# A new order of the attention stage's side work, and expert chunks of 352 and 288 rows

## The chip, the cores and the metric

The kernel runs on one core of one Trainium2 chip. Its time is the device time of one execution in microseconds (us), from the first to the last instruction and what lies around them; three runs gave 522.79, 523.56 and 525.09 us, median 523.56 us. Smaller is better.

## The reference

One block of a network on 16 sequences of 128 tokens with 256 features (2048 tokens), all in float32:

1. Sliding-window cross-attention: `x = x + tanh(g_xattn) * attention(layernorm(x), ctx, ctx)`. It has 16 heads of width 16. The tokens are read as two runs of 1024 in blocks of 128; a query sees keys of its own block and the one before, in a band of 129.
2. A mixture of experts: `x = x + tanh(g_ffn) * experts(layernorm(x))`. A router of 8 experts gives each token its two most probable ones. Each expert takes at most 640 of its tokens, in order, and computes `y = (silu(x W_g) * (x W_u)) W3` with 1024 hidden units; the results go back to the tokens, weighted by the router's probability.

```
logits = clip(xn @ Wr.T); probs = softmax(logits); top_p, top_i = top_k(probs, 2)
rank   = position of the token among those of its expert;  kept = rank < 640
gu = einsum('ecd,efd->ecf', buf, W12);  h = silu(g) * u
y  = einsum('ecf,edf->ecd', h, W3)
out[token] += y_slot * weight
```

For the inputs used, the reference's router sends 225, 328, 984, 337, 706, 204, 671 and 641 rows to experts 0 to 7. Four experts (0, 1, 3, 5) have fewer than 352 rows; the other four have more than 384 and fill all 640 slots. These are called light and heavy experts below.

## The kernel before, in words

Every engine has its own program, written out by hand in the order in which it runs; semaphores join them. There is no scheduler. The order of the calls in each `body` is the order of the instructions.

**Attention** (the first 200 us). Eight bodies, n = 0 to 7, treat two sequences each. A body has eight groups, g = 0 to 7, of four heads. The line numbers are those of the kernel before.

- TensorE computes `scores` (a mask matmul, L1306, and three fp32r products, L1309, into bank `S[g % 2]`), then transposes the probabilities of two groups earlier (`prob_columns`, L1319), then weighs the values of three groups earlier (`weigh_values`, L1333). `scores` of a group waits until ScalarE has done the exponentials of two groups earlier, since the bank is shared.
- VectorE takes the negated maximum of each row (`largest`, tile `nm`, L942), makes the low half of the probabilities (`low_probs`, tile `pT`, L947), and sums and scales the heads' output (`heads_out`, L956 and L958; `heads_scale`, tile `oN`, L966).
- ScalarE computes the exponentials (`exps`, tile `p`, four per group, L633) and the high half of the probabilities (`high_probs`, tile `pT`, L640).

Between these, each group has one piece of side work that belongs to another body: the next body's normalized inputs (`xn`, `xT`), keys (`k`), queries (`q`) and values (`vf`, `V`); the output projection of the body before (`oN` transposed by `output_columns`, L1341; copied to `oT`, L626; `project_out`, L1347); and layernorm and routing of the body before that (`x2_columns`, L1273 on TensorE, L587 on ScalarE, tile `xnT`; `logits`, L1281; the small VectorE operations from `clip_logits` to `slots`, whose end is `late`, `slot`, `pslot`, `slotu`, L925 to L937). Two banks serve all of it: `Xo` (outputs, x2, logits, ranks) and `Xp` (inputs, keys, queries, values). GpSimd runs the second layernorm (tile `xr`, L455 to L462) beside it and scatters the routed rows to memory with indirect DMAs.

**Experts** (from 227 us on). Expert e is done in one or two chunks of rows, `CHUNKS = ((0, 384), (384, 256))`. `up` computes for each of eight groups f of 128 hidden units two products (gate and up) over two halves of the features, each in three fp32r passes (high*high, low*high, high*low): 12 matmuls per f, 96 per chunk, the rows being the moving operand, so that each is 384 or 256 columns wide. ScalarE takes silu (L762), VectorE the product `hF` (L1162), ScalarE the high half `hH` (L742), VectorE the low half `hL` (L1166). `down` computes 128 rows of the output: the hidden values are the stationary operand, 128 columns of them, and W3 is the moving one, 256 wide; 24 matmuls for each tile t of rows. Meanwhile the next expert's weights are split into high and low halves (L727, L1133) and its rows transposed (`rows_columns`, L1481). `weigh` (L1183) scales a tile into `ysc`, and GpSimd adds it to the output with an indirect DMA (L549).

The second chunk runs only if the expert has more rows than the first chunk holds; a bit in `flags` says so, and each engine branches on it (`pe.If` at L1558).

## Time and profile before

| | us |
|---|---|
| median of three runs | 523.56 |
| the profiled execution, its own time | 523.19 |
| its span, first to last instruction | 521.3 |
| TensorE busy (matmul) | 478.3, 92% |
| VectorE busy | 351.9, 68% |
| ScalarE busy | 295.3, 57% |
| GpSimd busy | 189.6, 36% |

The span has three parts: attention to about 205 us, the last routing and the first rows' transposes to about 227 us, and the eight experts to 510 us, with the last addition behind them. Matmuls overlap, and the row of one gives its modelled length; how fast they follow each other is read from the starts of neighbouring rows. TensorE's granted clock is in the row PEclk, in tenths of full speed.

### The profile page before, as it was taken

What the parts mean: (1) busy time and instruction counts of PE and PEld (TensorE: products, weight loads), DVE (VectorE), ACT (ScalarE), POOL (GpSimd) and SP (SyncE); (2) the same over time, 40 slices, a digit from 0 to 9 for tenths busy, and PEclk for the clock granted to TensorE, in tenths of its full rate; (3) what the DMA queues carried; (4) which work ended last, traced back from release to release, by engine and by line L of the source; (5) the groups of instructions that cost most, each with busy time, mean ns of one, the idle gap of its engine ahead of it and who ended that gap; (6) DMA issues with size and microseconds to landing.
All of it is one profiled execution on the core that took longest, in us unless ns stands there. A gap on an engine that the chain in (4) does not pass through costs nothing.

```text
span 521.3 us, 10673 instructions
## 1 busy us (share of the span) xinstructions
PE 478.3 (92%) x3566; PEld 441.9 (85%) x3588; DVE 351.9 (68%) x864; ACT 295.3 (57%) x747; POOL 189.6 (36%) x257
## 2 busy tenths in 40 slices
PE   4899999999999886399999999999999999999991
PEld 3677888887878764399899999999999999999991
DVE  5697888889797997648776764675844858534340
ACT  5877878687778771427564643565633737324140
POOL 7527546686867576500303030112022030310302
PEclk9999999999999997589999999999999999999997
DMA  5999232414233511172757460465532464200111
GB/s 163 258 221 263 61 42 63 98 47 83 60 65 82 195 51 62 52 265 82 233 175 189 139 183 10 82 220 100 211 59 29 129 190 131 31 11 11 15 16 20
DMA packets 41650, 57.34 MB, mean 110 GB/s; under 512 B 3721, under 2 KB 38576, under 8 KB 39552
## 3 DMA queue, kind: packets, MB, share of 16 engines
q1 hardware_dynamic: 35008, 48.49, 31.9%
q0 software_dynamic: 6144, 8.07, 9.2%
q8 instruction: 28, 0.46, 0.4%
q10 hardware_dynamic: 448, 0.14, 0.2%
q14 instruction: 22, 0.18, 0.1%
HBM read 36.24 MB, written 16.72 MB: 102 GB/s over the span
## 4 chain that ended last, share of the span: by engine, by line
PE 56%; DVE 2%; issue 1%; DMA 0%; POOL 0%; another core or an unknown queue 0%; ACT 0%; DVEq 0%; POOLq 0%
PE bank L1487 18%; PE bank L1489 17%; PE bank L1488 17%; PE bank L1481 2%; PE bank L1415 1%; DMA expert_rows<-xr,slotu 0%; PE bank L1281 0%; POOL out_tokens L549 0%; PE bank L1273 0%; DVE xr L843 0%; DVE ysc L1183 0%; DVE xr L841 0%; DVE topi L884 0%; PE bank L1466 0%
## 5 line engine op out<-in xcount | busy, mean ns | idle before, releaser
L549 POOL DMA_INDIRECT out_tokens<-ysc,rows x32 | 49.8, 1558 | 243.9 <-DVE ysc L1183 237.3
L1487 PE MATMUL bank<-bXh,wh 128*128 128x384 f32 (+1 forms) x384 | 121.9, 318 | 1.5 <-issue 1.2
L1489 PE MATMUL bank<-bXh,wl 128*128 128x384 f32 (+1 forms) x384 | 121.8, 317 | 0.0
L1488 PE MATMUL bank<-bXl,wh 128*128 128x384 f32 (+1 forms) x384 | 121.8, 317 | 0.0
L762 ACT ACTIVATE sil<-bank 128x384 f32<-128x384 f32 (+1 forms) x96 | 43.8, 456 | 126.6 <-PE bank L1489 126.5
L1162 DVE TENSOR_TENSOR hF<-sil,bank 128x384 f32<-128x384 f32 (+1 forms) x96 | 49.0, 510 | 76.2 <-ACT sil L762 74.0
L633 ACT ACTIVATE p<-bank,nm 128x128 f32<-128x128 f32 x256 | 73.7, 384 | 25.1 <-DVE nm L942 25.0
L1487 PE MATMUL bank<-wh,hH 128*128 128x256 f32 x256 | 73.8, 288 | 0.3 <-DVE ysc L1183 0.3
L1488 PEld LDWEIGHTS bank<-bXl,wh 128*128 128x128 f32 x384 | 72.7, 189 | 1.3 <-issue 1.3
L1487 PEld LDWEIGHTS bank<-bXh,wh 128*128 128x128 f32 x384 | 72.7, 189 | 0.5 <-issue 0.5
L1489 PEld LDWEIGHTS bank<-bXh,wl 128*128 128x128 f32 x384 | 72.6, 189 | 0.0
L1489 PE MATMUL bank<-wh,hL 128*128 128x256 f32 x256 | 72.4, 283 | 0.0
L1488 PE MATMUL bank<-wl,hH 128*128 128x256 f32 x256 | 72.4, 283 | 0.0
L1309 PE MATMUL bank<-kM,q 128*128 128x512 f32 x192 | 67.0, 457 | 0.0
L1133 DVE TENSOR_TENSOR wl<-stage,wh 128x512 fp32r<-128x512 f32 x96 | 63.1, 685 | 3.1 <-ACT wh L727 1.6
L727 ACT ACTIVATE wh<-stage 128x512 fp32r<-128x512 f32 x96 | 56.6, 622 | 1.4 <-DMA stage<-in_w3T 1.4
L1487 PEld LDWEIGHTS bank<-wh,hH 128*128 128x128 f32 x256 | 49.0, 191 | 1.3 <-DVE ysc L1183 0.7
L942 DVE TENSOR_REDUCE nm<-bank 128x4 f32<-128x512 f32 x64 | 43.5, 680 | 8.6 <-PE bank L1309 8.5
L1166 DVE TENSOR_TENSOR hL<-hF,hH 128x384 fp32r<-128x384 f32 (+1 forms) x96 | 48.7, 507 | 0.7
L1488 PEld LDWEIGHTS bank<-wl,hH 128*128 128x128 f32 x256 | 49.1, 192 | 0.0
L1489 PEld LDWEIGHTS bank<-wh,hL 128*128 128x128 f32 x256 | 49.0, 192 | 0.0
L742 ACT ACTIVATE hH<-hF 128x384 fp32r<-128x384 f32 (+1 forms) x96 | 46.3, 482 | 0.9 <-DVE hF L1162 0.9
(144 smaller groups left out, 815.9 us busy)
## 6 DMA issues: line engine op xcount, KB each, us to landing
stage<-in_w12T SPq DMA_DIRECT2D x16, 1024.0 KB
stage<-in_w3T SPq DMA_DIRECT2D x8, 1024.0 KB
expert_rows<-padrow SPq DMA_DIRECT2D x8, 662.5 KB, 8.9
rows<-expert_rows SPq DMA_DIRECT2D x7, 662.5 KB, 4.2
kM<-k SPq DMA_DIRECT2D x62, 64.0 KB, 2.4
cT<-in_ctxT SPq DMA_DIRECT2D x8, 256.0 KB, 3.3
out_tokens<-x_all SPq DMA_DIRECT2D x8, 256.0 KB
x_all<-in_x SPq DMA_DIRECT2D x2, 640.0 KB, 5.6
```

The source lines that it names most:

```text
L549: pool.indirect_dma_start(out=out, out_offset=bass.IndirectOffsetOnAxis(rows[par][:, c, D + E:ROW].bitcast(U32), 0), in_=ysc[par][:, c, :] ...
L633: ins = act.activation(p32[g % 2][:, h, :], S[g % 2][:, h * T:(h + 1) * T], ACT.Exp, bias=nm[g % 2][:, h:h + 1])
L727: act.activation(Wh[par][:, k, q * QW:(q + 1) * QW], stage[s][:, q * QW:(q + 1) * QW], ACT.Copy)\
L742: act.activation(hH[c][:, f, :], hF[j % 2][:, 0:w], ACT.Copy).then_inc(act_hh, 1)
L762: act.activation(sil[j % 2][:, 0:w], Gb[j % 2][:, 0:w], ACT.Silu).then_inc(act_sil, 1)
L1133: dve.tensor_tensor(Wl[par][:, k, cols], stage[s][:, cols], Wh[par][:, k, cols].bitcast(F32), ALU.subtract)\
L1162: dve.tensor_tensor(hF[j % 2][:, 0:w], sil[j % 2][:, 0:w], Ub[j % 2][:, 0:w], ALU.mult).then_inc(dve_h, 1)
L1166: dve.tensor_tensor(hL[c][:, f - 1, :], hF[jj % 2][:, 0:w], hH[c][:, f - 1, :].bitcast(F32), ALU.subtract)\
L1309: ins = nc.tensor.matmul(S[g % 2][:, :], q2[par][:, sq, hq // 2, b * T:(b + 1) * T], kM[par][:, sk, GH * hq:GH * hq + GH, b * T:(b + 1) * ...
L1487: nc.tensor.matmul(out_ap, ah, bh, start=start, stop=False)
L1488: nc.tensor.matmul(out_ap, ah, bl, start=False, stop=False)
L1489: return nc.tensor.matmul(out_ap, al, bh, start=False, stop=stop)
```

## The change

Two independent edits.

**Order in the attention bodies.** On TensorE, `output_columns` of the body before moves from the end of group 0 to behind the scores of group 1, and `project_out` behind `weigh_values` of group 1. On VectorE, `low_probs` comes ahead of `heads_out`, and in group 0 ahead of `largest`; `keys_low` comes ahead of `largest` of group 3; the small router operations are spread anew, with `gate_columns` behind `slots`. On ScalarE, the keys move from group 3 (ahead of its exponentials) to group 2 (behind them), `x2_columns` behind these, `values1` from group 7 to the next body's group 0, and `values2` to group 1. The tile `slot` now lies in bank `Xo` in place of SBUF, so TensorE's next use of that bank waits for one operation more (`pslot`).

**Chunks.** `CHUNKS` becomes 352 and 288 rows; transposes and splits of the rows keep 384 and 256 (`TILED`). `hH` and `hL` become one tensor each. The third tile of rows straddles the chunks: a light expert computes its first 96 rows, with 96 stationary columns, and a heavy one computes all 128 after its second `up`. TensorE's branch now asks for fewer rows first.

```diff
-CHUNKS = ((0, 384), (384, 256))
+CHUNKS = ((0, 352), (352, 288))
+TILED = ((0, 384), (384, 256))
+SPLIT = 2
+REST = CHUNKS[0][1] - SPLIT * P
 # GpSimd, after the scatters
+            pool.memset(ysc[0][REST:P, SPLIT, :], 0.0).then_inc(spare_ok, 1)
+            pool.memset(ysc[1][REST:P, SPLIT, :], 0.0).then_inc(spare_ok, 1)
 # ScalarE, body
-                    if g == 7 and nxt:
-                        values(n + 1, Xp)
-                        values1(n + 1, 1 - par)
                     if (cur and g >= 2) or (prev1 and g < 2):
                         high_probs(G - 2, g % 2, not prev1 and g < 4)
                     if g == 0 and prev1:
+                        values1(n, par)
                         output_columns(SB * (n - 1), Xo)
-                    elif g == 2 and prev2:
-                        x2_columns(n - 2, Xo)
-                    elif g == 3 and nxt:
-                        keys(n + 1, Xp)
+                    elif g == 7 and nxt:
+                        values(n + 1, Xp)
                     if cur:
                         exps(G, g, not prev1 and g < 2)
...
+                    elif g == 2 and nxt:
+                        keys(n + 1, Xp)
+                    if g == 2 and prev2:
+                        x2_columns(n - 2, Xo)
 # VectorE, slots
-                dve.scalar_tensor_tensor(slot[:, a:b, :], late[:, a:b, :], LATE, rk, ALU.mult, ALU.add).then_inc(dve_rk, 1)
+                slot = bank[:, 2 * SB * E:2 * SB * E + (b - a) * E].rearrange("p (j e) -> p j e", e=E)
+                dve.scalar_tensor_tensor(slot, late[:, a:b, :], LATE, rk, ALU.mult, ALU.add).then_inc(dve_rk, 1)
 # TensorE, body
+                    if g == 1 and prev1:
+                        if prev3:
+                            pe.wait_ge(dve_rk, R_SLOT * (n - 3) + 3)
...
+                        output_columns(SB * (n - 1), Xo)
                     if (cur and g >= 2) or (prev1 and g < 2):
                         prob_columns(G - 2, g % 2, not prev1 and g < 4)
 # TensorE, expert
-                output_bank(e, 2, first)
-                down(e, par, 0, 2, range(FT))
-                with pe.If(more_rows(flags, e)):
+                with pe.If(fewer_rows(flags, e)):
+                    output_bank(e, SPLIT, first)
+                    down(e, par, 0, SPLIT, range(FT), REST)
+                with pe.Else():
                     up(i, par, 1, first)
-                    for t in range(CT0, CT):
+                    for t in range(SPLIT, CT):
                         output_bank(e, t, first)
                         down(e, par, 1, t, range(FT))
```

Three places show the moved instructions. The first is TensorE from group 0 to group 2 of an even body; `kM,q_0` are scores, `ident,p` the transposed probabilities, `ident,oN` the `output_columns`, `wo,oT` the projection. Before:

```order
L1309 MATMUL bank<-kM,q_0 128x512 x3
L1319 MATMUL bank<-ident,p_0 128x128 x4
L1234 MATMUL bank<-ident,xn 128x128 x4
L1333 MATMUL bank<-V_1,pT 128x50 x8
L1341 MATMUL bank<-ident,oN 128x128 x2
L1306 MATMUL bank<-causal,identb 128x512
L1309 MATMUL bank<-kM,q_0 128x512 x3
L1319 MATMUL bank<-ident,p_1 128x128 x4
L1347 MATMUL bank<-wo,oT 128x256 x2
L1333 MATMUL bank<-V_1,pT 128x50 x8
```

The same stretch of TensorE in the changed kernel, to the projection:

```order
L1327 MATMUL bank<-kM,q_0 128x512 x3
L1337 MATMUL bank<-ident,p_0 128x128 x4
L1252 MATMUL bank<-ident,xn 128x128 x4
L1351 MATMUL bank<-V_1,pT 128x50 x8
L1324 MATMUL bank<-causal,identb 128x512
L1327 MATMUL bank<-kM,q_0 128x512 x3
L1359 MATMUL bank<-ident,oN 128x128 x2
L1337 MATMUL bank<-ident,p_1 128x128 x4
L1351 MATMUL bank<-V_1,pT 128x50 x8
L1365 MATMUL bank<-wo,oT 128x256 x2
```

The transposes of `oN` now stand behind the next scores, and the projection behind the weighing.

The second place is VectorE from `largest` of group 7 to that of the next body's group 0 (`nm` is `largest`, `pT` is `low_probs`, `osum` to `oN` the heads, `late` to `slotu` the slots). Before:

```order
L942 TENSOR_REDUCE nm<-bank 128x4
L956 TENSOR_REDUCE osum<-bank 128x128
L958 RECIPROCAL bank<-bank 128x8
L966 TENSOR_TENSOR oN<-osum,bank 128x128
L947 SCALAR_TENSOR_TENSOR pT<-bank,pT 128x512
L925 TENSOR_TENSOR late<-bank,limit 128x16
L929 SCALAR_TENSOR_TENSOR slot<-late,bank 128x16
L931 TENSOR_TENSOR pslot<-pick,slot 128x32
L937 TENSOR_REDUCE slotu<-pslot 128x4
L942 TENSOR_REDUCE nm<-bank 128x4
```

And VectorE in the changed kernel, from the same `largest` on:

```order
L959 TENSOR_REDUCE nm<-bank 128x4
L964 SCALAR_TENSOR_TENSOR pT<-bank,pT 128x512
L973 TENSOR_REDUCE osum<-bank 128x128
L975 RECIPROCAL bank<-bank 128x8
L983 TENSOR_TENSOR oN<-osum,bank 128x128
L941 TENSOR_TENSOR late<-bank,limit 128x16
L946 SCALAR_TENSOR_TENSOR bank<-late,bank 128x16
L948 TENSOR_TENSOR pslot<-pick,bank 128x32
L954 TENSOR_REDUCE slotu<-pslot 128x4
L918 SCALAR_TENSOR_TENSOR xr<-lex,tg,lrc 128x2x8
L964 SCALAR_TENSOR_TENSOR pT<-bank,pT 128x512
L959 TENSOR_REDUCE nm<-bank 128x4 x2
```

`low_probs` moved ahead of the heads, `gate_columns` (`xr<-lex`) came in, and one more `low_probs` stands ahead of the next `largest`.

The third place is ScalarE in groups 2 and 3 (`pT` is `high_probs`, `p` the exponentials). Before:

```order
L640 ACTIVATE pT<-bank 128x512
L587 ACTIVATE xnT<-bank 128x512
L633 ACTIVATE p_0<-bank,nm 128x128 x4
L640 ACTIVATE pT<-bank 128x512
L606 ACTIVATE k<-bank,bqkv 128x256 x2
L633 ACTIVATE p_1<-bank,nm 128x128 x4
```

And in the changed kernel:

```order
L654 ACTIVATE pT<-bank 128x512
L647 ACTIVATE p_0<-bank,nm 128x128 x4
L620 ACTIVATE k<-bank,bqkv 128x256 x2
L601 ACTIVATE xnT<-bank 128x512
L654 ACTIVATE pT<-bank 128x512
L647 ACTIVATE p_1<-bank,nm 128x128 x4
```

The keys come one group earlier, and `xnT`, which the logits of group 3 read, now stands behind the exponentials and the keys.

## Rows read from the trace of the kernel before

**Rows 1.** The page: busy share of TensorE, and its granted clock in 40 slices.
```profile
PE 478.3 (92%) x3566; PEld 441.9 (85%) x3588; DVE 351.9 (68%) x864; ACT 295.3 (57%) x747; POOL 189.6 (36%) x257
PEclk9999999999999997589999999999999999999997
```
**Rows 2.** The page: the chain that ended last, by line.
```profile
PE bank L1487 18%; PE bank L1489 17%; PE bank L1488 17%; PE bank L1481 2%; PE bank L1415 1%; DMA expert_rows<-xr,slotu 0%; PE bank L1281 0%; POOL out_tokens L549 0%; PE bank L1273 0%; DVE xr L843 0%; DVE ysc L1183 0%; DVE xr L841 0%; DVE topi L884 0%; PE bank L1466 0%
```
**Rows 3.** Windows: length; busy us of PE, PEld, DVE, ACT, POOL; clock, DMA share, GB/s.
```profile
30.00:197.00 167.00, 159.10 (x1321) 132.76 (x1338) 142.36 (x396) 127.57 (x375) 108.01 (x144) 1.00 0.40 99
...
282.35:326.17 43.82, 43.82 (x325) 43.64 (x324) 25.57 (x53) 20.53 (x48) 8.61 (x6) 1.00 0.42 107
326.17:352.69 26.52, 26.52 (x181) 26.36 (x180) 18.46 (x35) 14.90 (x32) 3.73 (x4) 1.00 0.52 156
```
**Rows 4.** Groups by line and form, TensorE, 227 to 511 us.
```profile
L1487 PE MATMUL bank<-bXh,wh 128*128 128x384 f32 x256 | 85.7, 335 | 1.5 <-issue 1.2 <-DVE bXl L1140 0.3
...
L1487 PE MATMUL bank<-bXh,wh 128*128 128x256 f32 x128 | 36.2, 283 | 0.0
```
**Rows 5.** Timeline, TensorE, 384 columns; eleven rows of the same kind left out.
```profile
259.06 0.33 PE L1487 MATMUL bank<-bXh,wh 128*128 128x384 f32 x1
...
261.14 0.33 PE L1487 MATMUL bank<-bXh,wh 128*128 128x384 f32 x1
```
**Rows 6.** Timeline, TensorE, 256 columns (`down`); eleven rows left out.
```profile
307.09 0.28 PE L1487 MATMUL bank<-wh,hH 128*128 128x256 f32 x1
...
308.53 0.28 PE L1487 MATMUL bank<-wh,hH 128*128 128x256 f32 x1
```
**Rows 7.** Groups by line and form: VectorE's work in an expert.
```profile
L1133 DVE TENSOR_TENSOR wl<-stage,wh 128x512 fp32r<-128x512 f32 x96 | 63.1, 685 | 3.1 <-ACT wh L727 1.6 <-POOL lnv L539 1.4
...
L1162 DVE TENSOR_TENSOR hF<-sil,bank 128x384 f32<-128x384 f32 x64 | 35.5, 554 | 50.4 <-ACT sil L762 48.3 <-issue 2.1
L1166 DVE TENSOR_TENSOR hL<-hF,hH 128x384 fp32r<-128x384 f32 x64 | 35.3, 552 | 0.1
```
**Rows 8.** Groups by line and form: weight loads, fp32r (`down`) and fp16.
```profile
L1487 PEld LDWEIGHTS bank<-wh,hH 128*128 128x128 f32 x256 | 49.0, 191 | 1.3 <-DVE ysc L1183 0.7
...
L1333 PEld LDWEIGHTS bank<-V,pT 128*128 128x128 f16 x512 | 21.2, 97 | 11.5 <-DVE pT L947 6.0 <-issue 1.9
```
**Rows 9.** Timeline, TensorE: behind the first expert's branch.
```profile
257.50 0.33 PE L1487 MATMUL bank<-bXh,wh 128*128 128x384 f32 x1 [1.17 <-issue]
```
**Rows 10.** Waits, 30 to 197 us: us in total, times, longest.
```profile
PE bank L1333 <- DVE pT L947: 3.6, 7, 0.9
DVE k L979 <- ACT k L606: 6.6, 6, 1.1
ACT p L633 <- DVE nm L942: 24.1, 21, 2.0
```
**Rows 11.** Timeline where body 3 passes to 4, four engines.
```profile
106.29 0.38 PE L1333 MATMUL bank<-V,pT 128*128 128x50 bf16 x8 [0.54 <-DVE pT L947]
...
106.51 0.73 POOL L460 TENSOR_TENSOR xr<-xr,gab 128x256 f32<-128x256 f32 x1
106.55 0.73 DVE L931 TENSOR_TENSOR pslot<-pick,slot 128x32 f32<-128x32 f32 x1
...
107.42 0.68 DVE L942 TENSOR_REDUCE nm<-bank 128x4 f32<-128x512 f32 x1
...
108.14 1.15 ACT L633 ACTIVATE p<-bank,nm 128x128 f32<-128x128 f32 x4 [0.70 <-DVE nm L942]
...
109.38 1.04 PE L1309 MATMUL bank<-kM,q 128*128 128x512 f32 x3
```
**Rows 12.** Timeline, ScalarE, groups 2 and 3 of that body.
```profile
113.06 0.60 ACT L587 ACTIVATE xnT<-bank 128x512 f32<-128x512 f32 x1 [0.74 <-issue]
...
115.10 0.83 ACT L606 ACTIVATE k<-bank,bqkv 128x256 fp32r<-128x256 f32 x2
```
**Rows 13.** Waits of the whole span: TensorE's queries for VectorE's keys.
```profile
PE bank L1243 <- DVE k L979: 1.7, 2, 0.9
```

More of the change, by code:

```diff
@@ L131, in gated_block @@
         late = sb(pa, "late", [P, SB, E], F32)
-        slot = sb(pa, "slot", [P, SB, E], F32)
         pslot = sb(pa, "pslot", [P, K, SB, E], F32)
@@ L327, in _ @@
                 sp.wait_ge(scattered[s], 16 * K * SEQS // 2)
-            for (o, w), done in zip(CHUNKS, (ld_rows[0], ld_rows_rest)):
+            for (o, w), done in zip(TILED, (ld_rows[0], ld_rows_rest)):
                 if o > 0:
@@ L539, in _ @@
             pool.memset(lnv[:, :], 1.0).then_inc(pool_sent, 1)
+            for done in scattered:
+                pool.wait_ge(done, 16 * K * SEQS // 2)
+            pool.wait_ge(pool_sent, 1)
+            pool.memset(ysc[0][REST:P, SPLIT, :], 0.0).then_inc(spare_ok, 1)
+            pool.wait_ge(spare_ok, 1)
+            pool.memset(ysc[1][REST:P, SPLIT, :], 0.0).then_inc(spare_ok, 1)
+            pool.wait_ge(spare_ok, 2)
             pool.wait_ge(st_x2, 16 * NSB)
@@ L667, in body @@
                         queries(n + 1, 1 - par, Xp)
+                    if g == 4 and prev2:
+                        exps_of_logits(n - 2)
             def zero_low_keys(quarter):
@@ L1023, in body @@
                         stats1(*XCUT[g // 2:g // 2 + 2])
+                    if (cur and g >= 2) or (prev1 and g == 1):
+                        low_probs(G - 2, g % 2)
+                    if g == 4 and prev2:
+                        shift_logits(routed)
+                    elif g == 5 and prev2:
+                        sum_exps(routed)
+                    elif g == 6 and prev2:
+                        pick_experts(routed)
+                        guard_sum(routed)
+                        members(routed)
+                        invert_sum(routed)
                     if g in (1, 3) and prev1:
@@ L1031, in body @@
                         heads_scale(HPS * n + k, k, SB * n - 1 if prev1 else None)
-                    if (cur and g >= 2) or (prev1 and g < 2):
-                        low_probs(G - 2, g % 2)
-                    if g == 6 and prev2:
-                        members(routed)
-                        gate_columns(routed, par)
                     if g in (2, 6) and prev1:
@@ L1040, in body @@
                         slots(routed, par, Xo)
+                        gate_columns(routed, par)
             def zero_keys(par, part, half):
@@ L1176, in steps, with weigh @@
                         low(i + par, 1 - par, f)
-            def weigh(e, par, t, first):
+            def weigh(e, par, t, first, n=P):
                 if t == 0 and not (isinstance(e, int) and e < 2):
                     dve.wait_ge(expert_added, e - 1)
+                if t == SPLIT and isinstance(e, int) and e < 2:
+                    dve.wait_ge(spare_ok, e + 1)
                 dve.wait_ge(pe_out, CT * e + t + 1)
-                dve.tensor_scalar(ysc[par][:, t, :], Yb[(par + t) % 2][:, 0:D], rows[par][:, t, bass.ds(D + e, 1)], None, ALU.mult)\
+                dve.tensor_scalar(ysc[par][0:n, t, :], Yb[(par + t) % 2][0:n, 0:D], rows[par][0:n, t, bass.ds(D + e, 1)], None, ALU.mult)\
                    .then_inc(dve_ysc, 1)
@@ L1368, in body @@
                             values(n + 1, 1 - par, Xp)
-                    if g == 1 and prev1:
-                        project_out(SB * (n - 1), Xo)
-                    elif g == 2 and prev2:
+                    if g == 2 and prev2:
                         pe.wait_ge(dve_x2, SB * (n - 1) + 1)
@@ L1521, in up, with down @@
                     ins.then_inc(pe_gu, 1)
-            def down(e, par, c, t, parts):
-                o = t * P - CHUNKS[c][0]
+            def down(e, par, c, t, parts, n=P):
+                o = t * P
                 for f in parts:
-                    if t in (0, CT0):
+                    if t == c * SPLIT:
                         pe.wait_ge(dve_hl, 16 * e + FT * c + f + 1)
-                    ins = three(Yb[(par + t) % 2][:, 0:D],
-                                ((hH[c][:, f, o:o + P], hL[c][:, f, o:o + P]),
+                    ins = three(Yb[(par + t) % 2][0:n, 0:D],
+                                ((hH[:, f, o:o + n], hL[:, f, o:o + n]),
                                  (Wh[par][:, DC, f * D:(f + 1) * D], Wl[par][:, DC, f * D:(f + 1) * D])), f == 0, f == FT - 1)
@@ L1555, in expert @@
                     rows_columns(e + 1, 1 - par, i + 1 + par, 3)
-                output_bank(e, 2, first)
-                down(e, par, 0, 2, range(FT))
-                with pe.If(more_rows(flags, e)):
+                with pe.If(fewer_rows(flags, e)):
+                    output_bank(e, SPLIT, first)
+                    down(e, par, 0, SPLIT, range(FT), REST)
+                with pe.Else():
                     up(i, par, 1, first)
-                    for t in range(CT0, CT):
+                    for t in range(SPLIT, CT):
                         output_bank(e, t, first)
```

77 lines of the change are left out of this document (35 added, 42 removed).

## The prediction, made before the changed kernel ran

> **What bounds the kernel now.** I read the page first: TensorE is busy 92% of the span, at full clock but for two slices near the middle [rows 1], and the chain that ended last is TensorE's expert matmuls (L1487 to L1489) for over half of the span [rows 2]. Then the windows, since a mean hides stages. In a heavy expert TensorE is busy 43.82 of 43.82 us, in a light one 26.52 of 26.52, with VectorE and ScalarE far below, 18.46 and 14.90 us [rows 3]. So every nanosecond between two expert matmuls counts in full. In attention TensorE is busy 159.1 of 167 us, and VectorE 142.4 [rows 3]: these two are close, and what one waits for the other changes with the order. The waits name the joints: TensorE for `low_probs`, VectorE for ScalarE's keys, ScalarE's exponentials for the maxima [rows 10].
>
> **The chunks.** The row of a matmul (335 or 283 ns, [rows 4]) is longer than its pace; the pace is in the starts. Twelve matmuls of 384 columns take 261.14 - 259.06 = 2.08 us, 173.3 ns each [rows 5]; twelve of 256 take 308.53 - 307.09 = 1.44 us, 120 ns each [rows 6]. That is 0.4167 ns a column and a constant of 13.3 ns. Neither 352 nor 288 occurs; both lie between, so I take the line: 160 ns for 352, 133.3 ns for 288. The bounds are the neighbours: 352 can cost no more than 173.3 ns (the edit then gains nothing), and if 120 ns were a floor under a steeper line, it could be up to 7 ns less than the line says.
> - Light expert, four of them: 96 matmuls of `up` at 160 in place of 173.3 ns, 1.28 us less each, together 5.12 us.
> - Heavy expert, four: the first `up` is 96 x 13.3 = 1.28 us shorter, the second 1.28 us longer. Nothing.
> - `down`: 24 matmuls per tile before and after, with W3's 256 columns moving. For a light expert's third tile only the stationary side shrinks to 96 columns. I take the same 120 ns.
> - Does another engine stop TensorE from going faster? Per step of f it now needs 12 x 160 = 1.92 us; VectorE has hF, hL and one piece of the next weights, 554 + 552 + 685 = 1.79 us even at 384 columns [rows 7]. It fits, by 0.13 us, and more at 352.
> - The heavy third tile moves behind the second `up`. Its hidden values are ready, GpSimd's additions of 1.5 us keep pace with tiles of 24 x 120 = 2.88 us, and the tail behind the last tile is the same. Nothing. GpSimd's two clears lie in its idle time ahead of its first addition.
> - The branch: TensorE now decides ahead of the third tile. A heavy expert jumps over 24 matmuls and has only four row transposes queued to cover that (some 0.4 us). In before, a light expert jumps, under the cover of 2.9 us of queued matmuls; the first time there was nevertheless a gap of 1.17 us [rows 9], the other three had none. The bounds are 0 and 4 x (1.17 - 0.4) = 3.1 us, and below nothing about 0.5 us (the short wait for `ysc` ahead of that tile goes for heavy experts). I take 0, since a window with a jump is as full as one without [rows 3].
>
> The 96 columns are the place for a rule. A load of 128 fp32r columns shows 191 ns, one of fp16 97 ns [rows 8]: fp32r is loaded at the slow rate already. The Trainium skill, "TensorE: Matmul & The Clock Gate", on weight-path perf modes, says that the fast weight load is on when there are exactly 128 weights and the type is not FP32; by it, 96 columns would lose a fast load that 128 had. If fp32r had it, the sum would be about 2.6 us worse; by the row there is nothing to lose.
>
> **The order in attention.** Six bodies (2 to 7) have all the side work. I followed body 4 with the durations of its rows; zero is the start of its first scores, 103.8.
>
> Before, TensorE stalls 0.7 us at group 0 for `low_probs` of group 7 (0.54 visible, [rows 11]), since this stands behind the heads; 0.1 us at the scores of group 2, which follow the exponentials (108.14 + 1.15 to 109.38, [rows 11]); and 0.23, 0.15 and 0.1 us between the starts of neighbouring matmuls around the queries of group 4 and the projection of group 5. About 1.4 us a body.
>
> What goes: `low_probs` of group 7 comes about 1 us earlier, so the 0.7 us go; the keys on ScalarE end about 1 us earlier than 115.10 + 0.83 [rows 12], so VectorE's wait for them (6.6 us in six, [rows 10]) shrinks and the 0.5 us go. `pslot` took 0.73 us and ended at 107.28, just when GpSimd's L460 (106.51 + 0.73) did [rows 11]: two engines in one another's way. With `slot` in PSUM I take 0.2 us, like its neighbours.
>
> What comes: `low_probs` of group 0 (0.6 us) now stands ahead of the maxima on which ScalarE's exponentials wait. VectorE has no idle time here, so with the 0.5 us of `pslot` saved the maxima start at 3.4 to 4.1 us, against 107.42 - 103.8 = 3.6 [rows 11]. The exponentials end at 5.1 to 5.8; TensorE, no longer held at group 0, comes to the scores of group 2 at 4.6: a stall of 0.5 to 1.2 us where 0.1 was. Behind it ScalarE does `xT`, then the high half; VectorE waits for that, and the heads (1 us), formerly done in this pause, come behind it, so the maxima of group 2 end at 8.8 to 9.4. Then exponentials (1.05), keys (0.7) and only then `xnT` (0.5): it ends at 11.1 to 11.8, where the logits of group 3 would start at 10.3 to 10.9. A new stall of 0.9 us; before, `xnT` was done first, at 113.06 [rows 12], and there was none.
>
> Sum per body: 1.4 us of old stalls against 1.4 to 2.3 of new ones, 0 to +0.8; I take +0.25, times six, +1.5 us. Bodies 0 and 1 have no logits in the way and gain from the earlier keys: TensorE's queries stall 0.8 to 0.9 us in each [rows 13], most of which goes, -1.5 us. Attention together: 0, with bounds of -5 (old stalls go, the new ones stay hidden) and +5.
>
> `gate_columns` decides part of the spread. It reads two SBUF tiles, as `pslot` did, and now runs right behind `slotu`, beside GpSimd's L460 and L462; if blocked like `pslot`, it takes 0.5 us of the gain back. The Trainium skill, "SBUF — State Buffer", on the port pair that VectorE and GpSimd share, has it as an exclusive lock held for a whole instruction, taken by a VectorE operation with two SBUF inputs against a GpSimd one that reads SBUF. The rows of `pslot` agree. By this rule the upper ends above hold, +0.8 rather than 0.
>
> **Sum.** Against the profiled execution's own 523.19 us: -5.12 for the chunks, 0 for attention, 0 for the branch, 518.1. It ran 0.4 us under the median of the runs; from that median the same sum gives 518.4. I say 518.5.
>
> **Rivals.** 0.5% is 2.6 us, about what a measurement of this kernel can tell from no change: faster is below 520.9, slower above 526.2.
> - A, the forecast: chunks give 5.1 us, attention stays within 2 us. 516.5 to 520.5. Chance 0.48.
> - B, attention takes back 3 to 6 us: the logits' new wait and the later maxima show in full. For it: VectorE without idle time around the body's end, and `xnT` last in its row. Against: TensorE's old stalls do go. 521.5 to 524.5, say 522.6. Chance 0.20.
> - C, attention gains too: of 1.4 us of stalls per body 0.8 go, six times, 4.8 us. For it: VectorE's waits for keys were 1.1 us each. 513.5. Chance 0.15.
> - D, the narrow third tile or the heavy experts' jump costs 2.5 to 3 us: 521. For it the gap of 1.17 us; against it the full windows. Chance 0.11.
> - E, slower than before. Place: the scores of group 2. Mechanism: `gate_columns` is blocked, `low_probs` and maxima slip with it, TensorE waits at the weighing of group 1 (0.6), at the scores (0.6 more) and at the logits (1.0): some 2.7 us of stalls against 1.4. Six bodies, +8.1, less 5.1: 526.5. It turns slower when a body loses over 1.3 us. For it: [rows 11]; against: every term must be at its upper end. Chance 0.06.
>
> From these: faster 0.69 (A, C and half of D), same 0.25, slower 0.06. The range reaches from C's better half to B's middle, 514.0 to 522.8; A's own is 516.5 to 520.5.
>
> **What the new profile should show.** Starts of `up` matmuls 160 ns apart in first chunks and 133 in second ones; a light expert 25.2 us, a heavy one still 43.8, with no gap in front of its second `up`; `down` of the light third tile at 120 ns; `pslot` near 0.2 us; TensorE's wait for `low_probs` at group 0 gone, and waits for the exponentials at group 2 and for `xnT` at the logits in its place; bodies 23.2 to 24 us apart. I am wrong if light experts are not 1.3 us shorter, or if bodies change by more than 0.8 us.

## The result, and the profile after

The changed kernel took 528.91 us (median of six runs, 527.22 to 529.81) against 524.03 for the kernel before on the same chip: ratio 1.0091, 95% interval 1.0071 to 1.0112. It is slower; 518.5 was predicted, and the range ended at 522.8. The profiled execution took 528.68 us, with a span of 527.0 (before: 521.3).

The page of the changed kernel, busy shares and granted clock, then the chain by engine:

```profile
PE 476.7 (90%) x3588; PEld 440.1 (84%) x3588; DVE 347.2 (66%) x864; ACT 294.8 (56%) x747; POOL 190.0 (36%) x259
PEclk9999999999999997589799999998999999999997
...
PE 52%; issue 2%; DVE 2%; DMA 1%; POOL 1%; ACT 1%; another core or an unknown queue 0%; DVEq 0%; POOLq 0%
```

TensorE's share fell from 92% to 90% [rows 1], and the clock's digits have two new dips, a 7 and an 8, in the middle of the experts.

**What came as forecast.** Windows of the changed kernel, as in [rows 3]: attention, a heavy expert, a light one (expert 5).

```profile
30.00:197.00 167.00, 156.30 (x1311) 129.06 (x1309) 135.12 (x386) 126.27 (x369) 105.98 (x141) 1.00 0.40 99
286.40:330.22 43.82, 43.82 (x325) 43.75 (x323) 25.84 (x53) 20.50 (x48) 8.70 (x6) 1.00 0.43 107
404.07:429.21 25.14, 25.14 (x181) 24.99 (x179) 18.20 (x35) 14.44 (x32) 3.62 (x4) 1.00 0.54 163
```

The heavy expert is what it was, 43.82 us, and this light one 25.14 in place of 26.52. But attention is less full: 156.3 us of TensorE in 167, from 159.1. Groups by form, where [rows 4] had 384 and 256 columns:

```profile
L1505 PE MATMUL bank<-bXh,wh 128*128 128x352 f32 x256 | 84.9, 332 | 6.6 <-issue 6.3 <-DVE bXl L1156 0.3
...
L1505 PE MATMUL bank<-bXh,wh 128*128 128x288 f32 x128 | 38.0, 297 | 0.0
...
L1507 PE MATMUL bank<-wh,hL 128*96 128x256 f32 x32 | 8.9, 278 | 0.0
```

**What was not forecast** is in the first of these rows: 6.3 us of idle time with no releaser ("issue"). The timeline of TensorE shows where, behind expert 0's third tile:

```profile
254.94 0.28 PE L1506 MATMUL bank<-wl,hH 128*96 128x256 f32 x1
255.06 0.27 PE L1507 MATMUL bank<-wh,hL 128*96 128x256 f32 x1
258.50 0.63 PE L1505 MATMUL bank<-bXh,wh 128*128 128x352 f32 x1 [3.17 <-issue]
258.93 0.50 PE L1506 MATMUL bank<-bXl,wh 128*128 128x352 f32 x1
259.22 0.50 PE L1507 MATMUL bank<-bXh,wl 128*128 128x352 f32 x1
```

The same place behind expert 3:

```profile
355.32 0.27 PE L1507 MATMUL bank<-wh,hL 128*96 128x256 f32 x1
358.73 0.42 PE L1505 MATMUL bank<-bXh,wh 128*128 128x352 f32 x1 [3.13 <-issue]
```

From start to start these are 3.44 and 3.41 us, where 0.12 is normal. The matmuls behind the first gap then follow 0.29 us apart (258.93 to 259.22), not 0.16: the window behind it shows TensorE at half of its clock, 1.2 of 2.4 GHz (0.50), and the next one the way back. Behind the second gap the clock fell only 1.3 us later, so its window has a mean of 0.71.

```profile
258.50:262.00 3.50, 3.50 (x12) 3.50 (x13) 0.00 (x0) 0.00 (x0) 1.54 (x1) 0.50 0.96 274
262.00:266.00 4.00, 4.00 (x20) 4.00 (x19) 1.37 (x3) 1.65 (x4) 0.00 (x0) 0.69 0.30 69
...
358.70:362.00 3.30, 3.27 (x15) 3.28 (x16) 0.00 (x0) 0.38 (x2) 0.00 (x0) 0.71 0.36 42
```

What TensorE's sequencer did at the time stands in its branch records. They are not counted as busy, so no timeline has them; a query by source line gives their durations (ns, min/median/max). Of the changed kernel, the jumps over the long side of experts 0, 1, 3 and 5:

```profile
L1574 PEldq COMPARE_BRANCH  x1: 5226/5226/5226, 253.1 to 253.1; - x1
L1574 PEldq COMPARE_BRANCH  x1: 299/299/299, 284.3 to 284.3; - x1
L1574 PEldq COMPARE_BRANCH  x1: 4602/4602/4602, 353.4 to 353.4; - x1
L1574 PEldq COMPARE_BRANCH  x1: 174/174/174, 427.1 to 427.1; - x1
```

And all eight branches of the kernel before, with the first matmul behind the jump at 252.6:

```profile
L1558 PEldq COMPARE_BRANCH  x8: 68/148/373, 252.6 to 490.7; - x8
```
```profile
254.60 0.34 PE L1487 MATMUL bank<-bXh,wh 128*128 128x384 f32 x1
```

Two jumps take about 5 us in place of 0.3. The sequencer is some 2 us ahead of the matmuls, in the kernel before (252.6 to 254.60) as in the changed one (253.1 to 255.06): so much of a jump is covered, and the rest is the gap.

**The sum of the profiled executions**, in us. Experts: the four light ones -1.4 each, -5.5 (26.52 to 25.14; 5.1 of it are the columns), the wait for `ysc` in the last expert -0.6, the two gaps 3.3 + 3.3, the slow matmuls behind them 2.9 + 1.6 (expert 1's `up` takes 18.25, from 258.50 to 276.75, in place of 15.4, expert 4's 17.0), the old gap [rows 9] -1.4; +3.6 together. From the first expert matmul to the last it is +3.5. Attention and routing: the first expert matmul is at 229.3 in place of 227.2, +2.1. Together that is the 5.7 us of the span, to 0.1.

In attention the stalls are those that the prediction named. Waits from 30 to 197 us, as in [rows 10], then TensorE and `pslot` where body 3 passes to 4, as in [rows 11]:

```profile
PE bank L1324 <- ACT p L647: 2.1, 6, 0.4
PE bank L1299 <- ACT xnT L601: 3.9, 5, 0.8
...
PE bank L1351 <- DVE pT L964: 1.4, 3, 0.9
DVE k L996 <- ACT k L620: 4.1, 6, 0.7
```
```profile
107.08 0.19 DVE L948 TENSOR_TENSOR pslot<-pick,bank 128x32 f32<-128x32 f32 x1
...
107.41 0.23 DVE L918 SCALAR_TENSOR_TENSOR xr<-lex,tg,lrc 128x16 f32<-128x16 f32 x1
...
110.06 0.39 PE L1324 MATMUL bank<-causal,identb 128*128 128x512 bf16 x1 [0.37 <-ACT p L647]
...
116.10 0.61 PE L1299 MATMUL bank<-wr,xnT 128*128 128x8 f32 x4 [0.78 <-ACT xnT L601]
```

From start to start, 0.66 us at the scores of group 2 and 0.95 at the logits in each full body; the 0.7 us for `low_probs` are gone. A body takes 23.5 to 23.6 us where it took 23.15. The first logits already come 1.3 us later than before, at 69.04 for 67.75.

### The profile page after: what moved, and what is told of

Same layout as the page of the kernel before. It is cut to its first block, busy times and chain, and to the rows that moved or that the text cites. A ratio compares the mean times of both kernels' runs of the same rounds, so it can differ in the third digit from the quotient of the medians.

```text
span 527.0 us, 10704 instructions
## 1 busy us (share of the span) xinstructions
PE 476.7 (90%) x3588; PEld 440.1 (84%) x3588; DVE 347.2 (66%) x864; ACT 294.8 (56%) x747; POOL 190.0 (36%) x259
## 4 chain that ended last, share of the span: by engine, by line
PE 52%; issue 2%; DVE 2%; DMA 1%; POOL 1%; ACT 1%; another core or an unknown queue 0%; DVEq 0%; POOLq 0%
PE bank L1505 17%; PE bank L1506 17%; PE bank L1507 17%; PE bank L1499 1%; DMA stage<-in_w3T 1%; PE bank L1433 1%; POOL expert_rows L482 1%; ACT wh L743 0%; DVE wl L1149 0%; DMA expert_rows<-xr,slotu 0%; POOL out_tokens L563 0%; DVE osum L973 0%; DVE x_all L991 0%; DVE st L844 0%
## 5 line engine op out<-in xcount | busy, mean ns | idle before, releaser
L1505 PE MATMUL bank<-bXh,wh 128*128 128x352 f32 (+1 forms) x384 | 122.9, 320 | 6.6 <-issue 6.3
L1506 PE MATMUL bank<-bXl,wh 128*128 128x352 f32 (+1 forms) x384 | 122.3, 318 | 0.0
L1507 PE MATMUL bank<-bXh,wl 128*128 128x352 f32 (+1 forms) x384 | 122.2, 318 | 0.0
L1178 DVE TENSOR_TENSOR hF<-sil,bank 128x352 f32<-128x352 f32 (+1 forms) x96 | 47.9, 499 | 79.7 <-ACT sil L778 75.7
L1505 PE MATMUL bank<-wh,hH 128*128 128x256 f32 (+1 forms) x256 | 73.1, 286 | 0.0
L1506 PE MATMUL bank<-wl,hH 128*128 128x256 f32 (+1 forms) x256 | 72.3, 282 | 0.0
L1507 PE MATMUL bank<-wh,hL 128*128 128x256 f32 (+1 forms) x256 | 72.2, 282 | 0.0
L1505 PEld LDWEIGHTS bank<-wh,hH 128*128 128x128 f32 (+1 forms) x256 | 48.0, 188 | 0.5 <-DVE ysc L1201 0.2
L1182 DVE TENSOR_TENSOR hL<-hF,hH 128x352 fp32r<-128x352 f32 (+1 forms) x96 | 47.7, 497 | 0.7
L1506 PEld LDWEIGHTS bank<-wl,hH 128*128 128x128 f32 (+1 forms) x256 | 48.1, 188 | 0.0
```

The source lines that it names most:

```text
L1178: dve.tensor_tensor(hF[j % 2][:, 0:w], sil[j % 2][:, 0:w], Ub[j % 2][:, 0:w], ALU.mult).then_inc(dve_h, 1)
L1182: dve.tensor_tensor(hL[:, f - 1, o:o + w], hF[jj % 2][:, 0:w], hH[:, f - 1, o:o + w].bitcast(F32), ALU.subtract)\
L1505: nc.tensor.matmul(out_ap, ah, bh, start=start, stop=False)
L1506: nc.tensor.matmul(out_ap, ah, bl, start=False, stop=False)
L1507: return nc.tensor.matmul(out_ap, al, bh, start=False, stop=stop)
```

## The experiments

Each ratio is to the kernel before on the same chip, with its 95% interval.

### The two edits apart

**order_only** has the attention's hunks of the diff and none of the chunks'.

> The kernel before with the new attention order alone (with slot in PSUM), chunks and branches as before. Theory A (the order costs about 2 us, the rest of the loss is in the experts): bodies 23.5 us apart instead of 23.2, TensorE stalls 0.6 us ahead of the scores of group 2 and 0.9 us ahead of the logits, experts unchanged at 282.7 us; time 2 us above before, 525.5 to 526.5. Rival B (the order is the whole loss, since it also shifts the experts): 529.

527.77 us, ratio 1.0066 (1.0047 to 1.0086): above theory A's range and below B's 529. Its jumps are before's, its stalls those of the changed kernel (0.66 and 0.95 us a body), and its experts take 282.8 us, as before's do, so B's reason is excluded.

**chunks_only** has the chunks and the branch.

> The kernel before with the chunks of 352 and 288 and the new branches alone, attention order as before. Theory A (TensorE's jump over the long side behind a light expert's third tile finds its target not yet fetched): gaps of 3.3 us behind the third tile of experts 0 and 3, and 1.7 to 2.5 us in the up of the experts after them, as in the changed kernel; 3 to 4 us above before, 527. Rival B (the gaps come from the new attention order): no gaps, 5 us below before, 518.8.

525.04 us, ratio 1.0022 (0.9995 to 1.0050). The gaps are there, 4.08 and 3.27 us, behind jumps of 5.86 and 4.57 us. 1.0066 x 1.0022 = 1.0088: the two edits add up to the change's 1.0091, within their intervals. So the order costs some 3.5 us, and the chunks, which save 5.1 us of matmuls, give it all back at the branch; alone, they are not shown to be slower than before.

### The attention's new stalls

**xnt_first** is order_only with `x2_columns` again ahead of the exponentials of group 2:

```diff
+                    elif g == 2 and prev2:
+                        x2_columns(n - 2, Xo)
...
-                    if g == 2 and prev2:
-                        x2_columns(n - 2, Xo)
```

> The new attention order alone (order_only, 527.8), with ScalarE's copy to xnT put back ahead of the exponentials of group 2; the keys stay behind them. Theory A (xnT last in its row makes the logits wait): the 0.94 us ahead of the logits in six bodies goes; up to 5.6 us less, 522 to 524. Rival B (VectorE's and ScalarE's total work sets the pace of a body, the wait only moves): bodies still 23.5 us apart, 527.8.

**max_first** is order_only with `low_probs` of group 0 again behind `largest`:

```diff
-                    if g == 0 and prev1:
-                        low_probs(G - 2, g % 2)
                     if cur:
                         largest(G, g)
+                    if g == 0 and prev1:
+                        low_probs(G - 2, g % 2)
```

> The new attention order alone (order_only, 527.8), with low_probs of group 0 put back behind the maxima. Theory A (the maxima of group 0 are late, TensorE waits 0.6 us for the exponentials ahead of the scores of group 2): that wait shrinks by 0.5 us, the wait at the logits by as much or not at all; 2 to 5 us less, 523 to 526. Rival B (TensorE then waits for low_probs at the weighing of group 1 instead): 527 to 528.

They took 523.54 us (1.0002, 0.9987 to 1.0017) and 523.17 us (1.0003, 0.9989 to 1.0016). Each takes away one stall (the logits'; most of the scores') and is back at before's time.

**best_order** makes both edits.

> Only the attention part of the change, with two steps put back: on ScalarE the half of the layernorm's transposes (xnT) again ahead of the exponentials of group 2, and on VectorE low_probs of group 0 again behind the largest. Each of the two alone brought the kernel back to the time before (523.5 and 523.2, from 527.8). Theory: the two waits (0.95 us at the logits, 0.66 us at the scores of group 2) are separate, each was worth some 4 us, but the wait that each removal leaves (scores of group 2; weighing of group 1, 0.71 us) is the time that the other would give. With both out a body loses the old wait for low_probs only in part: 22.8 to 23.1 us a body, 521 to 522.5 us. Rival: VectorE itself sets the body by then, so both together give no more than one alone: 523 to 523.6.

523.34 us, 1.0008 (0.9992 to 1.0024): the rival. Both new stalls are gone, and the old one for `low_probs` is back, one group later. TensorE's timeline of best_order, at the weighing of group 1:

```profile
108.24 0.36 PE L1334 MATMUL bank<-V,pT 128*128 128x50 bf16 x8 [0.68 <-DVE pT L949]
```

A body takes 23.15 us, as in before, and its stalls sum to about 1.4 us in both. In the orders tried here, what VectorE and ScalarE do between two exponentials comes late somewhere, and the order chooses where; that no other order does better is not shown.

**slot_sbuf** is order_only with `slot` in SBUF again, and the new place of `gate_columns` kept:

```diff
-                slot = bank[:, 2 * SB * E:2 * SB * E + (b - a) * E].rearrange("p (j e) -> p j e", e=E)
+                slot = slot_s[:, a:b, :]
```

> The new attention order alone (order_only, 527.8), with slot back in SBUF. Theory A (two SBUF inputs make pslot wait for GpSimd's running operation): pslot 0.4 to 0.7 us again where it meets one, 0.2 where it does not, and the maxima of group 0 later by that; 0 to 3 us more, 528 to 531. Rival B (pslot's length came from its place in the order): 0.2 us, 527.8.

529.87 us, 1.0132 (1.0104 to 1.0161): 2.1 us above order_only by the medians, 3.5 by the ratios. The timeline of VectorE and GpSimd in slot_sbuf:

```profile
107.63 0.74 POOL L460 TENSOR_TENSOR xr<-xr,gab 128x256 f32<-128x256 f32 x1
...
107.95 0.46 DVE L934 TENSOR_TENSOR pslot<-pick,slot_s 128x32 f32<-128x32 f32 x1
...
108.45 0.73 POOL L462 TENSOR_TENSOR xr<-xr,beb 128x256 f32<-128x256 f32 x1
...
108.55 0.66 DVE L904 SCALAR_TENSOR_TENSOR xr<-lex,tg,lrc 128x16 f32<-128x16 f32 x1
```

`pslot` ends with GpSimd's L460 (108.41 and 108.37), and `gate_columns`, which starts 0.1 us behind L462, ends with it (109.21 and 109.18). In the changed kernel `gate_columns` starts at 107.41, ahead of the second of the two GpSimd operations (107.56), and takes 0.23 us; `pslot`, with one input in PSUM, takes 0.19 us (107.08) in the middle of the first one (106.75 to 107.48). The Trainium skill ("SBUF — State Buffer", the two sides of SBUF) has this as an exclusive lock, and the rows agree: 0.3 us for `pslot` and 0.4 for `gate_columns`, by the phase of two engines. A body takes 24.2 us in place of 23.5. Of the parts of the order that were tried alone, `slot` in PSUM is the one that pays.

### The gap: its length or its place?

**long_first** turns the branch of the changed kernel round:

```diff
-                with pe.If(fewer_rows(flags, e)):
-                    output_bank(e, SPLIT, first)
-                    down(e, par, 0, SPLIT, range(FT), REST)
-                with pe.Else():
+                with pe.If(more_rows(flags, e)):
                     up(i, par, 1, first)
...
+                with pe.Else():
+                    output_bank(e, SPLIT, first)
+                    down(e, par, 0, SPLIT, range(FT), REST)
```

A light expert now jumps over the long side ahead of its third tile, with only four transposes queued.

> The changed kernel with the long side of TensorE's branch first: a light expert jumps over it at once to its third tile, with only four transposes queued. Theory A (place of the jump's target): the jump now starts some 50 instructions earlier in the piece, so for expert 0 the target is already there: gap under 0.5 us instead of 3.4; 521 to 526. Rival B (the short side first was the better choice, since the jump is covered by 2.9 us of queued matmuls): gaps of 4 us or more at all light experts, above 530.

532.0 us, 1.0176 (1.0146 to 1.0207). The time fell on B's side, and A's gap under 0.5 us did not come; but the gaps, 4.90 and 5.78 us, are at experts 0 and 3 alone, not at all light ones. Expert 0's is the one that tells:

```profile
L1574 PEldq COMPARE_BRANCH  x1: 374/374/374, 251.5 to 251.5; - x1
```
```profile
252.95 0.28 PE L1507 MATMUL bank<-wh,hL 128*96 128x256 f32 x1
257.85 0.37 PE L1505 MATMUL bank<-wh,hH 128*96 128x256 f32 x1 [4.63 <-issue]
```

The same long jump takes 0.37 us, nine matmuls run behind its target, and then TensorE stands for 4.9 us in the middle of a tile where nothing is waited for. So it is not the jump's length alone. (Expert 3's gap stands at its jump, a record of 6.03 us.)

**split_branch** is chunks_only with `up` in an `If` of its own, so that no jump is longer than before's:

```diff
+                with pe.If(more_rows(flags, e)):
+                    up(i, par, 1, first)
                 with pe.If(fewer_rows(flags, e)):
...
                 with pe.Else():
-                    up(i, par, 1, first)
                     for t in range(SPLIT, CT):
```

> The new chunks alone (chunks_only, 525.0), with TensorE's branch in two: the second up in one If, then short or long down in another. A light expert jumps over 192 instructions, does its third tile, and jumps over 144, never over 336 at once. Theory A (a jump beyond the 16 KB pieces present waits for two fetches one after the other): no gap over 1.5 us, the time falls by 4 to 7 us, 518.5 to 521. Rival B (every light jump in the first pass costs a fetch, however far): the two gaps stay at 3 us or more, or four appear, 524 to 530.

524.79 us, 1.0023 (1.0001 to 1.0044): nothing gained, and theory A fell. Gaps of 2.67 us at experts 0 and 3, behind records of 4.45 and 3.96 us of jumps over only 148 and 158 instructions.

The two gaps are alike, and the clock behind them is not. Windows behind the first and the second:

```profile
255.40:259.20 3.80, 3.80 (x24) 3.80 (x25) 1.03 (x3) 0.98 (x2) 1.54 (x1) 1.00 0.91 268
352.20:356.00 3.80, 3.80 (x17) 3.80 (x18) 0.31 (x1) 0.97 (x2) 0.64 (x1) 0.68 0.43 55
```

So a gap of this length can cost the clock or not. That goes with the spread of one kernel's executions: of split_branch's ten, four took 522.0 to 522.8 us at a mean granted clock of 0.967 to 0.970, and six 524.6 to 526.2 at 0.960 to 0.964.

**after_pad64** is the changed kernel with code moved and nothing else: 64 matmuls of 8 columns where TensorE waits for the scatters, 128 instructions with their weight loads.

```diff
+            for _ in range(64):
+                nc.tensor.matmul(O[0][:, 0:E], onesb[:, :], member[:, 0, :], start=True, stop=True)
             for s in range(2):
                 pe.wait_ge(scattered[s], 16 * K * SEQS // 2)
```

> The changed kernel with 64 more matmuls of 8 columns (results unused) ahead of TensorE's wait for the scatters, where it sat idle for 4.3 us. Every later TensorE instruction lies 128 instructions further on in its program; the experts' instructions are the same. Theory A (where the jumps lie relative to the 16 KB pieces in which instructions are fetched decides): the gap of 3.4 us behind expert 0 goes or others appear; the jump of expert 0 takes 0.1 to 0.4 us in place of 5.2. Time between 519 and 527, and the pattern of gaps changes. Rival B (a jump behind the short side is slow for itself, or the 96 columns are): the same gaps of 3.4 us behind experts 0 and 3, 529.

527.07 us, 1.0050 (1.0021 to 1.0079), at the upper end of A's range. Expert 0's jump is fast, expert 1's now slow, and expert 3's as slow as it was (4.57 us). The window behind its gap of 3.36 us is at full clock:

```profile
L1576 PEldq COMPARE_BRANCH  x1: 346/346/346, 254.0 to 254.0; - x1
L1576 PEldq COMPARE_BRANCH  x1: 4451/4451/4451, 279.8 to 279.8; - x1
```
```profile
358.58:362.40 3.82, 3.82 (x24) 3.82 (x25) 0.85 (x2) 0.98 (x2) 0.00 (x0) 1.00 0.33 39
```

### The theory, and its two tests

The DMA part of the page has the fetching of instructions as a queue of its own, of the changed kernel:

```profile
q8 instruction: 29, 0.48, 0.4%
```

29 packets of 16,384 bytes each, so 256 instructions of 64 bytes; one comes each time TensorE enters a new piece of 256, 2 to 4 us after, so it holds the piece behind that. The places are counted in TensorE's compiled program, from its start. By these places the stall of long_first lies exactly between the weight load at place 255 of piece 15 and its matmul at place 0 of piece 16; and so does before's old gap [rows 9]. That gives the theory: the piece being run and the next one are there, and the one behind is asked for only when the next is entered; it can be run some 4.5 to 6 us later. A jump waits if it ends two pieces on, or in the next one when its own was entered less than that ago; and so does straight code that reaches a boundary too soon behind a jump. Places are counted piece.place:

| kernel, expert | jump from | into | its record, us | gap, us |
|---|---|---|---|---|
| before, 0 | 14.199 | 15.235 | 0.37 | 1.51 at 16.0 |
| changed, 0 | 14.201 | 16.30 | 5.23 | 3.44 |
| changed, 1 | 17.137 | 18.222 | 0.30 | none |
| changed, 3 | 23.53, entered 1.4 us earlier | 24.150 | 4.60 | 3.41 |
| after_pad64, 0 | 15.73 | 16.158 | 0.35 | none |
| after_pad64, 1 | 18.9, just entered | 19.94 | 4.45 | 2.87 |
| after_pad64, 3 | 23.181 | 25.22 | 4.57 | 3.36 |

The Trainium skill, "Runtime: NRT & Kernel Launch", on instruction fetch mechanics, states the blocks of 256 instructions, and that a taken branch out of a window of two forces a fetch before anything continues. The rows agree for jumps forward. The jump at the end of the loop, six pieces back, is one that the window of two does not hold, and it took 0.23 us (358.1). The page gives two sizes for TensorE's store, 2048 instructions and two blocks; the loop over experts 2 to 5 (1464 instructions) fetched 7 pieces to the end of its first pass and none in its second (no row of that queue from 363 to 437 us), which only the larger allows. Expert 5's jump, of 0.17 us, lies in that second pass.

**chunks_placed** is chunks_only with 96 such matmuls at the scatters, and 70 in expert 2's short side, which never runs with these inputs:

```diff
+                    for _ in range(spare):
+                        nc.tensor.matmul(Yb[par][:, 0:E], onesb[:, :], member[:, 0, :], start=True, stop=True)
                     down(e, par, 0, SPLIT, range(FT), REST)
...
-                expert(i, 0, False, False)
+                expert(i, 0, False, False, spare=70)
```

> The chunks and the branch of the change alone, and TensorE's code shifted: 96 tiny matmuls (8 columns) where TensorE waits for the scatters anyway, and 70 more in expert 2's short side, which never runs. Counting TensorE's program in pieces of 256 instructions, the light experts' jumps over the long side then go from place 137 of piece 15 into piece 16 (expert 0), from 73 of 18 into 19 (expert 1), and from 129 of 24 into 25 (expert 3); in the change alone they go from piece 14 into 16, 17 into 18, and from place 53 of 23, entered 1.3 us earlier, into 24. Theory of the pieces (only the next one is there, and it needs 5 to 6 us from when the one ahead of it is entered): the gaps of 4.1 and 3.3 us and the slow matmuls behind them (1.6 and 1.7 us) go, at most 1 us stays behind expert 0's jump. 516 to 518.5 us, from 525.0. Rival, the length of the jump or its being taken right behind another branch makes the gap, wherever it lies: 524 to 526.

516.31 us, ratio 0.9867 (0.9840 to 0.9893). The three jumps, and the windows behind the first and the third, at full clock:

```profile
L1575 PEldq COMPARE_BRANCH  x1: 346/346/346, 250.6 to 250.6; - x1
L1575 PEldq COMPARE_BRANCH  x1: 290/290/290, 276.1 to 276.1; - x1
L1575 PEldq COMPARE_BRANCH  x1: 281/281/281, 345.2 to 345.2; - x1
```
```profile
255.75:262.00 6.25, 6.25 (x39) 6.25 (x40) 4.56 (x10) 3.75 (x10) 2.04 (x1) 1.00 0.69 199
347.27:355.00 7.73, 7.73 (x50) 7.73 (x49) 4.44 (x9) 3.72 (x8) 2.88 (x2) 1.00 0.57 63
```

One gap is left, 0.51 us, behind the 17th matmul of expert 1's `up`, at the first places of piece 17. Code that does no work is worth 8.7 us here (525.04 to 516.31), 8.1 by the ratios. The added matmuls did nothing else that the trace shows: the first expert matmul comes at 226.75 us, in chunks_only at 226.69.

**best_placed** has the attention of best_order besides, as the whole change put right.

> The whole change with the two steps of the attention put back (best_order) and the code shifted as in chunks_placed. If both parts add up as they did in the change: best_order's time, less 5.1 us for the columns, 0.5 us for the wait for ysc and 1.4 us for the old gap behind expert 0's jump, plus 1 us for the added matmuls: 515 to 517 us. Rival, the jumps stay as slow as in the change: 523.

515.96 us, 0.9858 (0.9830 to 0.9885): the fastest, though not measurably faster than chunks_placed.

**before_pad26** tries the theory on the kernel before: the loop of after_pad64 with `range(26)`, nothing else.

> The kernel before, with nothing but 26 tiny matmuls (52 instructions) more where TensorE waits for the scatters. By the count its jumps behind expert 0 and expert 3 then end two pieces further (from place 251 of piece 14 into 16, from 208 of 22 to the first places of 24), where they ended one piece further before. Theory of the pieces: each jump's record goes from 0.35 to some 5 us, of which 2.9 us lie under queued matmuls; a gap of 2.2 us at each, and slow matmuls for 1.5 to 2 us behind it, against one gap of 1.5 us before: 528 to 531 us. Rival, only the change's longer jump or its second branch is slow: 523.5 to 524.5.

525.83 us, 1.0037 (1.0022 to 1.0051). Slower, but by less than half of what was expected, because only the first of two jumps went as the count said. The two records, then the gap behind the first and the window behind it:

```profile
L1560 PEldq COMPARE_BRANCH  x1: 5101/5101/5101, 253.7 to 253.7; - x1
L1560 PEldq COMPARE_BRANCH  x1: 340/340/340, 355.5 to 355.5; - x1
```
```profile
255.61 0.28 PE L1489 MATMUL bank<-wh,hL 128*128 128x256 f32 x1
258.97 0.41 PE L1487 MATMUL bank<-bXh,wh 128*128 128x384 f32 x1 [3.08 <-DVE wl L1133]
...
258.97:262.00 3.03, 3.03 (x13) 3.03 (x14) 0.00 (x0) 0.00 (x0) 1.54 (x1) 0.71 0.80 291
```

The gap of 3.36 us bears a releaser's name, `wl`, that was done long before; the branch record says what it was. It is longer than the 2.2 us expected, since some 2 us of matmuls were queued and not 2.9. Expert 3's jump ends by the count at the very first place of piece 24, and was free. In split_branch too, some 14 instructions ran beyond a boundary in the loop before the sequencer stood still.

The count itself is a likely reason. The compiled program also holds labels, which mark the targets of jumps, and the count above takes them as instructions. Ahead of the two stalls at exactly 16.0 (before and long_first) stand two labels of the experts; ahead of chunks_placed's, between 17.0 and 17.1, three; ahead of split_branch's jump at 24.14, 19; ahead of before_pad26's target, nine. If a label takes no place, the boundaries of the last three lie 1, 17 and 7 places further on than by the count that fits the first two: chunks_placed's stall is met exactly, split_branch's jump at 24.14 is still in piece 23, and so is before_pad26's target. The packets agree: before_pad26 has 28, as many as before, though with its labels it would begin one piece more (7436 instructions, 29.05 pieces, against 28.84). No run was made to test this. No jump of chunks_placed ends near enough to a boundary to depend on it.

## Why the prediction was wrong

- **The branch: the step that failed.** "I take 0, since a window with a jump is as full as one without", with bounds up to 3.1 us. It cost 11.1 us (gaps and slow matmuls) less the old gap's 1.4. The windows were full because in before each jump happened to end in the piece that was at hand; that says nothing of a kernel whose code lies elsewhere. The bounds looked at the heavy experts' jump, which was new and short; what changed for the light ones is that their jump, of 341 instructions for 292, now ended two pieces on (expert 0), or in the next one too soon (expert 3). The cover was 2 us before and after, not the 2.9 that the prediction took. The upper bound was no bound either: 4 x (1.17 - 0.4) takes a cover off a gap that, as it was read, had stood behind a cover already. Not one rival had the right place.
- **The one clue, misread.** The gap of 1.17 us [rows 9] was priced as the cover that was missing at a jump. It lay nine matmuls of `up` behind it, at a boundary of the code. A gap with no releaser at a place where the program waits for nothing was the thing to explain.
- **The clock.** The prediction had no term for it. A gap of 1.5 us (before) left the granted clock at 1.00; behind the two of 3.4 us it fell to 1.2 GHz, and the matmuls there took 2.9 and 1.6 us more. It need not fall: behind expert 3's gap of 3.27 us in chunks_only and of 3.36 in after_pad64 it stayed at 1.00. What decides between the two is open.
- **The chunks: right.** Matmuls of 352 columns follow each other at 160 ns, of 288 at 133, and 5.1 us were saved, as chunks_placed shows in full. `down` with 96 stationary columns takes 24 x 119.9 = 2.88 us, as [rows 8] had suggested. The Trainium skill's rule on 128 weights ("TensorE: Matmul & The Clock Gate", weight-path perf modes) changed nothing here. The heavy expert's jump had no gap (D had the wrong jump).
- **Attention: right mechanism, wrong size.** Both new stalls came where they were worked out, 0.66 us (0.5 to 1.2 forecast) and 0.95 (0.9). The old ones went. But a body is 0.4 us slower rather than 0.25, and the first bodies, which were to win 1.5 us, lost 1.3 (the first logits at 69.04 for 67.75; in order_only, with the same attention, at 70.11): +2.1 us in the profile of the changed kernel, and +3.5 in order_only by its ratio, against 0. Of the other cases B, 3 to 6 us, is what the order alone came to. Why the first bodies lost is open.
- **`pslot` and `gate_columns`: right.** 0.19 us, and 0.23 us unblocked. Rival E's mechanism exists (slot_sbuf), but not in the changed kernel; E's size came true by another cause.
- **Slips in the working**, which change nothing above. [rows 1] has three slices below full clock near the middle (7, 5, 8), not two. The new stalls of a body, 0.5 to 1.2 and 0.9 us, make 1.4 to 2.1, not 2.3. E's 2.7 against 1.4 us in six bodies is 7.8, not 8.1. C's own 513.5 lies below the range that was to start in C's better half.

## What to carry to other kernels

A branch in a long unrolled program has a price that depends on where its target lies in the instruction stream: here 0.3 us or 5 us, and the clock behind it. Look at the branch records and at gaps without a releaser, and when an edit moves code ahead of a branch or lengthens a side, measure it at a second placement before judging the edit. The chunks came out at 1.0022 in one placement and at 0.9867 in another. Of those 1.3% about 1 us is the old gap, which before might lose by a better placement too; that was not tried. Where stalls of two engines take turns, as in these bodies, taking each away alone shows whether they add up; here they did not.

## What the runs showed of the hardware

- TensorE's instructions arrive in pieces of 16,384 bytes, each fetched once (29 packets in the changed kernel); one is usable some 4.5 to 6 us after the piece ahead of it is entered (records of 4.45 to 6.03 us where a jump ends two pieces on or its own piece was just entered). In straight code the wait was seen only close behind a jump: a piece of 256 instructions otherwise lasts longer (14.8 us for piece 20 of the kernel before, from 309.25 to 324.01).
- A loop body of 1464 instructions ran its second pass without a fetch (no packet from 363 to 437 us).
- The granted clock behind gaps of TensorE: 0.68 in the 3.8 us behind one of 2.67 us and 1.00 behind another of 2.67 us (both split_branch), 0.50 in the 3.5 us behind one of 3.44 us, 0.50 in the 4.2 us behind one of 4.90 us (long_first); 1.00 behind one of 3.36 us (after_pad64), one of 3.27 us (chunks_only), one of 1.51 us (before) and one of 0.51 us (chunks_placed).
- A VectorE operation with two SBUF inputs (`pslot`) took 0.46 to 0.73 us where a GpSimd operation was under way, and ended with it; with one input in PSUM it took 0.19.
